# Layer two of a three-layer graph convolution: the adjacency builds move from a tile's slots 1 to 8 to its slots 10 to 17

## The reference, cut to what matters

```python
src = jnp.concatenate([edge_index[0], loops]); dst = jnp.concatenate([edge_index[1], loops])
deg = jax.ops.segment_sum(jnp.ones_like(dst, dtype=x.dtype), dst, num_segments=n)
dinv = jnp.where(deg > 0, jax.lax.rsqrt(deg), 0.0)
norm_edge = dinv[src] * dinv[dst]
h = x
for W, b in ((W1, b1), (W2, b2), (W3, b3)):
    # _gcn_layer: h = h @ W; agg = segment_sum(h[src] * norm_edge[:, None], dst); agg + b
    h = jax.nn.relu(_gcn_layer(h, W, b, src, dst, norm_edge, n))
x = _layernorm(x + h, axis=-1)
```

## Time and profile before

| | us |
|---|---|
| median of 3 runs | 2998.45 |
| the runs | 2988.33 to 2999.68 |
| the profiled execution | 2973.64 |
| its span, first to last instruction | 2971.9 |
| layer two's sums, first to last of 49 | 1208.23 to 2371.01 |

### The profile page before, as it was taken

One profiled execution on the slowest core, in us unless ns is written; L12 is line 12 of the kernel. 1 busy time (PEld: TensorE's weight loads), 2 busy tenths in 40 slices (PEclk: granted clock), 3 DMA queues, 4 the chain that ended last, 5 costly groups with the idle time before them and its releaser, 6 DMA issues.

```text
span 2971.9 us, 39305 instructions
## 1 busy us (share of the span) xinstructions
PE 2399.8 (81%) x12137; PEld 1634.2 (55%) x12138; DVE 982.6 (33%) x1127; ACT 719.0 (24%) x1501; POOL 1701.7 (57%) x1768
## 2 busy tenths in 40 slices
PE   6866777787777778788878788878888789889888
PEld 6744556565555555334334343434433378878787
DVE  8865222222222211323334333334232223223232
ACT  6411222222122121122121212212121123323232
POOL 4366655555455554656666566666666555555553
PEclk8778899899999899988989899889999899999998
DMA  5445555454454555667767676666767566656563
GB/s 180 138 125 190 161 156 162 144 152 147 143 151 134 154 153 157 194 200 227 220 209 233 201 234 206 220 204 211 230 205 247 162 197 190 181 171 193 171 182 104
DMA packets 219974, 537.81 MB, mean 181 GB/s; under 512 B 38444, under 2 KB 88483, under 8 KB 219827
## 3 DMA queue, kind: packets, MB, share of 16 engines
q0 software_dynamic: 117216, 365.08, 42.5%
q1 hardware_dynamic: 83955, 123.53, 12.0%
q10 hardware_dynamic: 18656, 47.20, 4.9%
HBM read 448.05 MB, written 87.61 MB: 180 GB/s over the span
## 4 chain that ended last, share of the span: by engine, by line
PE 48%; another core or an unknown queue 25%; issue 12%; DVE 6%; ACT 5%; ACTq 1%; POOL 1%; DMA 1%; DVEq 0%; POOLq 0%; SPq 0%
PE ps_acc L1642 10%; PE ps_d L1642 8%; PE ps_o L1691 6%; PE ps_acc L1638 5%; PE ps_d L1741 4%; PE ps_h L1682 2%; PE ps_T L1729 2%; PE ps_T L1730 2%; ACT rows_r L1422 2%; PE ps_h L1729 2%; PE ps_h L1730 2%; ACT big L1404 1%; PE ps_l L1712 1%; PE ps_e L1712 1%
## 5 line engine op out<-in xcount | busy, mean ns | idle before, releaser
L727 POOL DMA_INDIRECT rows<-table,idx x1249 | 1202.4, 963 | 788.3 <-issue 369.4
L944 DVE SCALAR_TENSOR_TENSOR sel<-ps_e,firsts,dstT 128x1152 f32<-128x1152 f32 (+1 forms) x214 | 302.5, 1414 | 1211.6 <-PE ps_acc L1642 365.0
L1642 PE MATMUL ps_acc<-rows,sel 128*128 128x512 f32 (+2 forms) x1496 | 641.6, 550 | 61.9 <-DVE acc L1029 21.7
L727 POOL DMA_INDIRECT rows<-table_parts,idx x483 | 456.5, 945 | 380.5 <-PE ps_acc L1638 160.1
L1642 PE MATMUL ps_d<-rows,sel 128*128 128x512 f32 (+2 forms) x1190 | 527.0, 557 | 14.8 <-DMA rows<-table,idx 11.3
L1642 PEld LDWEIGHTS ps_acc<-rows,sel 128*128 128x128 f32 x1496 | 284.1, 211 | 206.9 <-issue 170.0
L1691 PE MATMUL ps_o<-low,hT 128*128 128x512 f32 (+1 forms) x784 | 292.9, 519 | 57.8 <-ACT hT L1347 29.9
L1638 PE MATMUL ps_acc<-rows,sel 128*128 128x256 bf16 (+1 forms) x1533 | 254.5, 283 | 59.6 <-DVE acc L1029 33.1
L1642 PEld LDWEIGHTS ps_d<-rows,sel 128*128 128x128 f32 x1190 | 210.3, 199 | 147.0 <-issue 127.1
L1691 PEld LDWEIGHTS ps_o<-low,hT 128*128 128x128 f32 x784 | 154.1, 202 | 178.3 <-issue 132.1
L1741 PE MATMUL ps_d<-big 128*128 128x256 bf16 x1470 | 239.4, 281 | 10.9 <-issue 10.9
(11 more groups left out here) (195 smaller groups left out, 2244.6 us busy)
## 6 DMA issues: line engine op xcount, KB each, us to landing
built<-big SPq DMA_DIRECT2D x84, 384.0 KB
low<-built ACTq DMA_DIRECT2D x84, 384.0 KB
rows<-table,idx POOLq DMA_INDIRECT x1249
table<-made SPq DMA_DIRECT2D x49, 256.0 KB
acc<-table SPq DMA_DIRECT2D x49, 256.0 KB
built<-big SPq DMA_DIRECT2D x28, 416.0 KB
low<-built ACTq DMA_DIRECT2D x28, 416.0 KB
table_parts<-big SPq DMA_DIRECT2D x24, 384.0 KB
```

The costliest lines, as they stand in the source:

```text
L727: pool.indirect_dma_start(out=to, out_offset=None, in_=its[0:nodes, :], in_offset=bass.IndirectOffsetOnAxis(ap=idx[:, of, k:k + 1], axis=0 ...
L944: v.scalar_tensor_tensor(to[:, k:k + FRONT, :], numbers.unsqueeze(1).broadcast_to([P, FRONT, P]), firsts[:, bass.ds(t, 1)], dstT[:, bass.d ...
L1642: return mm(to[:, 0:w], sel[:, k, :], rows_of[phase][:, k, 0:w] if first is None else first, start=start, stop=stop)
```

## The change

In layer two the pairs stand in front of the positions 10 to 17 of a window, in place of 1 to 8 (`start = SLOTS - PAIRS`). On DVE, `add_self` and `one_hots` come behind `take_sum`, the indices and the second half of `sel` of the same window, in place of between the first half of `sel` and `take_sum`. On ACT, all eight copies come behind the relu. Layer one keeps its order; layer three has no builds.

```diff
--- before.py
+++ after.py
@@ -1113,10 +1113,14 @@
                     base = base_of(t)
                     next_base = None if last else base_of(next_tile)
                     prepare(n, t, base, 0, sel_parts if in_parts else sel)
-                    if whole is not None:
-                        add_self(*whole)
-                    if hots is not None:
-                        one_hots(*hots)
+                    def built_parts():
+                        if whole is not None:
+                            add_self(*whole)
+                        if hots is not None:
+                            one_hots(*hots)
+
+                    if phase == 0:
+                        built_parts()
                     if dense is not None:
                         finish_dense(*dense)
                     if units is not None:
@@ -1127,6 +1131,8 @@
                     elif phase < 2:
                         v.tensor_copy(idx[:, 1 - odd, :], early_src[:, :]).then_inc(idx_ready, 1)
                     prepare(n, t, base, 1, sel_parts if in_parts else sel)
+                    if phase > 0:
+                        built_parts()
 
                 def to_next(phase):
                     n = nth_of_windows(phase + 1, 0)
@@ -1374,8 +1380,8 @@
                     if built_half is not None:
                         keep_pairs(*built_half, range(*gs))
 
-                keep(0, PAIRS // 2)
                 if phase == 0:
+                    keep(0, PAIRS // 2)
                     keep_aggT(s, aggT[:, 0:C], 0)
                     keep(PAIRS // 2, PAIRS)
                     relus(s)
@@ -1383,7 +1389,7 @@
                     act.wait_ge(turned, s + 1)
                     for m in range(KH):
                         relu_T(ps_T[:, m * P:(m + 1) * P], b2T, m)
-                    keep(PAIRS // 2, PAIRS)
+                    keep(0, PAIRS)
                 make(phase, t, s, per)
 
             def keep_keys():
@@ -1858,7 +1864,7 @@
                     for o in range(ROUND):
                         half = half_in(o)
                         steady(1, ROUND * i + o + 1, PLACES[1],
-                               building(2 * (DENSE_1 + len(STARTS) * i + half[0]) + half[1]) if half is not None else None,
+                               building(2 * (DENSE_1 + len(STARTS) * i + half[0]) + half[1], SLOTS - PAIRS) if half is not None else None,
                                ps=ps_sums[(WINDOWS[1] + o + 1) % 2])
                 left = ROUND * ROUNDS + 1
                 with pe.Fori(0, (T - 1 - left) // 2) as i:
```

## The result

The change takes the kernel from a median of 2999.06 us (4 runs, 2988.33 to 3000.67) to 3139.89 us (4 runs, 3116.44 to 3147.26): a ratio of 1.0466, 95% interval 1.0422 to 1.051. I had predicted 2995, with a range that ended at 3045. The profiled execution took 3135.68 us, of which 3133.9 are its span: 162.0 us more than before.

A forecast was written before the change was run, and what follows sets the result against it. PE's waits before the pairs and POOL's gathers were taken to bound layer two; -161.7 + 73 + 86 + 11 + 18 - 29 = -3 us on 2998 gave 2995 us, range 2945 to 3045.

The forecast's parts named there:

- What bounds layer two: Layer two: PE idles 161.7 us before the pairs, 4.5 us a half; POOL's gathers and the chain between tiles also bound windows.
- the floor of 19.9 us: POOL in layer two: 15.9 gathers a window at 1.25 us each, below which POOL can't go.
- Whatever lateness exists in the second half is now waited for: PE's pairs at positions 10 to 17: late signals add 2.4 us once a window, 86 us over 36 windows.
- the 11 and 18 beside it: Added waits: 11 us for DVE's one-hots, 18 us for last pairs with no slot between them, 0.5 us a window.
- my upper bound of 4.5: Upper bound in us for late waits at positions 10 to 17: what six answers cost today at the early positions.
- The waits at the transposes: PE at position 5: the chain between tiles now meets PE there, 2.0 us a window, 73 us for 36 windows.
- -29: Overlap of late waits with each other: a third of the 86 us taken off, so some transpose wait goes.
- The one-hots: DVE, behind the sum: PE waits 0.3 us a window on average for them, 11 us, against 10.2 that leave.
- rival 3: DVE's one-hots come late: half of 36 windows cost 2 us each, 36 us, 3031 us; chance 0.06.
- Rival 2: Late answers at positions 10 to 17 delay the window's end and POOL's gathers: slower, 3040 us; chance 0.26.
- 2995 + 58 - 8: Rival 2's sum: forecast, plus no overlap (+29) and dearer answers (+29), less the share already waited at the transposes.
- Rival 1: Early waits at the pairs go and late ones don't come: 23.4 us a window, 47 us less, 2951; chance 0.32.

## Why the prediction was wrong

- **What bounds layer two.** Right as far as it went: PE's waits in front of the pairs, its taking turns with POOL, the floor of 19.9 us by POOL's issues. With the signals on time a window with builds takes 20.3, on that floor.
- **"Whatever lateness exists in the second half is now waited for. I take the average that DVE sees, 2.4 us once in a window": the step that failed.** The mechanism was right. The size, 86 us with the 11 and 18 beside it, stood for what measured 240: 6.7 us a half, above even my upper bound of 4.5. I had sized lateness as one waiter sees it, who asks once in a window. A chain of six answers asks again each time it gets one, so it can't step over a bout as a single wait can: in the fence above the answers come at 1454.5, 1457.3, 1462.9 and 1468.5. And 2.4 us was an average over slot 8 alone. The trace of before could have said more: the signal of the window's last slot, for which the sum on DVE waits, has 28 records there, 2.5 us behind the slot's drawn end on average and 12.2 at most (0.01 on average over 42 with signals on time). By that the average was fair for one waiter, and what was mis-sized is how often a window pays it.
- **The clock was not in the sum.** PE's same instructions took 44 us more. In the bout above PE's idle of 4.36 us was followed by a slot of 1.96 us in place of 1.05, at a granted clock of 0.50: such waits are paid for again on the next matmuls.
- **The waits at the transposes** were oversized: 73 predicted, 32.6 measured (22.7 with pairs at 6 to 13). A window whose lateness was waited for in its second half starts with less of it, which I had booked apart as -29; the two together, 44, are near enough.
- **The one-hots** in time: 2.3 us (11 predicted); rival 3 did not happen. ACT's and DVE's orders are worth nothing that can be told, as I had costed them, shown by undoing each alone.
- **Rival 2** had the direction and the place (waits of 4 us or more a window at positions 10 to 17, POOL's waits from 187.4 to 319.9 us), but priced the answers at the early positions' 4.5 us, and for half the windows only: 3040 us, where the ratio makes it 3138 from the median that I started at. Its own terms, 2995 + 58 - 8, add up to 3045, not 3040, which changes nothing here.
- **Rival 1**, that the early waits go and no late ones come, is what happens to the waits with signals on time, and it still gains nothing (1.0007), since there the early waits don't exist either: in the kernel before with more signals, in the on-time set, no row of PE waiting at a pair is left.

The Trainium skill (Perfetto Trace Analysis, section Tensor Engine Instruction) separates the drawn end of a matmul, an estimate, from the moment at which PSUM acknowledges and the signal goes out. The runs here show how far apart the two can be: 0.04 us for pair 0, 10.3 us for pair 4 of the same window. They also show that it isn't only drawn so: the semaphore records and the starts of the copies have the same lateness, and the time of one kernel differs by 520 us between the two conditions.

**What stays open.** What puts a chip in either condition, and what holds the signals. The runs exclude the bytes of the gathers, the number of PE's signals, and the orders of ACT and DVE. That gathers under way have to do with it rests on the counts (0 of 51 against 140 of 237); no run took the gathers away, or changed their number, at the same number of pairs, and with signals on time the same gathers hold nothing up. In the trace of after, 28 of the 502 gaps between PE's recorded signals lie between 5.5 and 6.0 us, with 1 in the half microsecond below and 2 in the one above, as between the signals of pairs 2, 3 and 4 above (5.59 and 5.63); nothing here tells why. All executions on record carry the profiler's clock and span, so whether the recording, which loses most of its semaphore records in the late condition alone, has a part in it is open too.

## What to carry to other kernels

Put an answer that one engine needs from another where it is needed late (another buffer), and leave the stretch in which signals come late to work that runs on without one: in the late condition the same eight pairs cost 2% at positions 6 to 13 and 4.3% to 4.7% at 10 to 17, and a third bank gave 1% at the early positions. Lateness seen by an engine that waits once (2.4 us a window here) can be far below what a chain of handshakes pays (6.7 us). Run the kernel before beside every candidate, in the same set: here the chip's condition moved the time by 520 us, and the change moved it by nothing or by 4.7% depending on that.

## What the runs showed of the hardware that I had not expected

- One kernel takes 2,980 or 2,457 us by the chip's condition, each steady within a set (spread up to 1.7% and 0.5%). With signals on time PE is busy for 91% of the span at a clock of 0.97, otherwise 78% to 81% at 0.88 to 0.91.
- In the late condition PE's signals alone are late (188 of 503 recorded ones by over 1 us); of 712 of ACT, DVE, POOL and SP none is.
- PE's completion signals can lie 10.3 us behind the drawn end of the matmul, and two of them then came 0.06 us apart.
- Halving the gathered bytes, from 188 to 115 GB/s, changes the time by less than 0.5% in both conditions. With signals on time it is POOL's 1.25 us a gather that sets the rate (841 of 858 us); in the late condition it is PE's waits.
